# Two fused cross attentions on one core: x, context and weights turned before the launch, and layer two's maxima fused with their row term

## The reference

```python
# layer one (L0)
q = emb @ Wq + bq;  k = latent @ Wk + bk;  v = latent @ Wv + bv
w = softmax(q @ k.T / sqrt(512), axis=1)          # over the queries
x = w @ v + emb
n = (x - mean(x)) * rsqrt(var(x) + 1e-6);  x = n * gamma + beta
# layer two (L1)
Q = x @ Wq + bq;  K = ctx @ Wk + bk;  V = ctx @ Wv + bv
p = softmax(Q @ K.T / sqrt(512), axis=-1)
out = x + (p @ V) @ Wo + bo
```

## Time and profile before

| | |
|---|---|
| median of 3 runs | 739.02 us (738.49 to 739.14) |
| profiled execution, its own time | 739.57 us |
| span of the profile | 737.5 us, so 2.07 us lie outside it |
| PE busy | 690.4 us (94%) |
| DVE busy | 623.4 us (85%) |
| ACT busy | 422.5 us (57%) |
| POOL busy | 489.0 us (66%) |
| DMA | 49.50 MB, mean 67 GB/s |

### The profile page before, as it was taken

One profiled execution on the slowest core, in us unless ns is written; L12 is line 12 of the kernel. 1 busy time (PEld: TensorE's weight loads), 2 busy tenths in 40 slices (PEclk: granted clock), 3 DMA queues, 4 the chain that ended last, 5 costly groups with the idle time before them and its releaser, 6 DMA issues.

```text
span 737.5 us, 12580 instructions
## 1 busy us (share of the span) xinstructions
PE 690.4 (94%) x4107; PEld 596.5 (81%) x4107; DVE 623.4 (85%) x1282; ACT 422.5 (57%) x1009; POOL 489.0 (66%) x391
## 2 busy tenths in 40 slices
PE   8997989899998989999998999999899999989886
PEld 6875978788897878888797888889788878978775
DVE  4896797988979798897979889797989989797964
ACT  3644747556475656646574755647375574847432
POOL 0177758768484876858487685848669584857571
PEclk9999999999999999999999999999999999999999
DMA  8802004040300304040120404022040402101002
GB/s 287 284 1 86 2 10 134 1 142 0 133 9 34 108 0 142 0 142 0 49 93 0 142 0 142 0 65 77 0 142 0 142 0 91 51 0 58 1 1 114
DMA packets 30336, 49.50 MB, mean 67 GB/s; under 512 B 2160, under 2 KB 10352, under 8 KB 30320
## 3 DMA queue, kind: packets, MB, share of 16 engines
q1 hardware_dynamic: 30320, 49.29, 19.9%
HBM read 32.51 MB, written 16.78 MB: 67 GB/s over the span
## 4 chain that ended last, share of the span: by engine, by line
PE 55%; DVE 32%; ACT 5%; issue 4%; POOL 2%; DMA 1%; DVEq 0%; SPq 0%; POOLq 0%
PE bank L384 43%; PE bank L391 11%; DVE n L1003 6%; DVE neg L955 5%; DVE mx L949 3%; DVE top L952 3%; DVE stats L992 3%; DVE pc_lo L802 2%; DVE e L1109 2%; ACT e L702 2%; DVE wc_lo L802 1%; DVE x_odd L987 1%; DVE x_even L987 1%; ACT prod L709 1%; ACT wc_hi L631 1%
## 5 line engine op out<-in xcount | busy, mean ns | idle before, releaser
L1181 POOL TENSOR_TENSOR prod<-n,u_b 128x512 f32<-128x512 f32 x64 | 81.6, 1296 | 5.5 <-ACT prod L715 5.5
L800 DVE SCALAR_TENSOR_TENSOR y_lo<-bank,terms,y_hi 128x512 fp32r<-128x512 f32 x64 | 45.6, 748 | 37.5 <-ACT y_hi L629 37.5
L1210 POOL TENSOR_TENSOR r<-r,beta_b 128x512 f32<-128x512 f32 x60 | 75.7, 1289 | 0.0
L1203 POOL TENSOR_TENSOR r<-n,gamma_b 128x512 f32<-128x512 f32 x60 | 75.5, 1286 | 0.0
L1173 POOL TENSOR_TENSOR rstd<-var_eps,minus_half 128x2 f32<-128x2 f32 x32 | 22.4, 699 | 78.9 <-DVE var_eps L999 78.8
L629 ACT ACTIVATE y_hi<-bank,terms 128x512 fp32r<-128x512 f32 x64 | 42.0, 680 | 51.6 <-PE bank L384 51.5
L631 ACT ACTIVATE xT_hi<-bank 128x512 fp32r<-128x512 f32 x64 | 33.0, 605 | 67.0 <-PE bank L391 67.0
L702 ACT ACTIVATE e<-bank,neg 128x256 f32<-128x256 f32 x64 | 29.7, 469 | 52.7 <-DVE neg L955 52.7
L1142 POOL TENSOR_TENSOR cn_even_lo<-ctxn,cn_even_hi 128x1024 fp32r<-128x1024 f32 x8 | 19.2, 2394 | 56.3 <-ACT cn_even_hi L739 56.3
L384 PE MATMUL bank<-wvo_hi,pc_hi 128*128 128x512 f32 x128 | 52.2, 408 | 4.2 <-DVE pc_lo L802 4.2
L384 PE MATMUL bank<-xT_hi,wqk_hi 128*128 128x512 f32 x128 | 52.6, 411 | 2.0 <-DVE xT_lo L802 2.0
(11 more groups left out here) (197 smaller groups left out, 2514.4 us busy)
## 6 DMA issues: line engine op xcount, KB each, us to landing
out_dram<-r SPq DMA_DIRECT2D x15, 1024.0 KB, 5.1
x_even<-in_x_dram SPq DMA_DIRECT2D x8, 1024.0 KB, 7.1
...
x_odd<-in_x_dram SPq DMA_DIRECT2D x8, 1024.0 KB, 6.9
...
wq_sb<-in_L_xattn_Wq_dram SPq DMA_DIRECT2D x1, 1024.0 KB, 11.9
```

The source lines that it names most:

```text
L800: i = dve.scalar_tensor_tensor(dst, src, bias, high.bitcast(F32), ALU.add, ALU.subtract)
L1181: pool.tensor_tensor(prod[j % 2][:], N[:, j, :], u_b[1][:], ALU.mult).then_inc(prod_ready, 1)
L1203: pool.tensor_tensor(r[:, j, :], N[:, j, :], gamma_b[:], ALU.mult).then_inc(scaled_ready, 1)
L1210: pool.tensor_tensor(r[:, j, :], r[:, j, :], beta_b[:], ALU.add).then_inc(resid_ready, 1)
```

## The change

The host lays out transposed copies: `x_turned` and `ctx_turned` (per pair, partition = column), and Wq, Wk, Wv transposed; `columns` holds six bias vectors by partition. TensorE no longer turns x, ctx or weights. x arrives a second time as `x_raw` (1 MB a pair), ctx as `c_raw` (512 KB, in the buffer E1). ScalarE rounds `x_raw` in two halves (`round_xT`) and VectorE subtracts (`cut_xT`), both for the pair ahead and inside the previous iteration; ScalarE rounds `c_raw` (`round_cT`) and GpSimd subtracts (`cut_cT`). The bias vectors are products on TensorE with one column each (`term_columns`) in place of VectorE's dot products. In `maxima1` one tensor_scalar adds r1s and takes the maximum, writing into E1, and the exponential then reads E1. In GpSimd's order `row_products` 2, 3 moves behind `add_w_lo`, in ScalarE's `row_terms` 2, 3 behind wc. PSUM is used in rounds of 7 banks.

```diff
             def project(it, name, source, wqk, src):
                 dst = [begin(it, name, c) for c in range(KC)]
                 for k in range(KD):
-                    wait_emptied(pe, it, source, k)
+                    if source == "nT":
+                        wait_emptied(pe, it, "nT", k)
+                    elif k % 2 == 0:
+                        pe.wait_ge(xT_lo, it.times(2, k // 2 + 1))
...
+            def term_columns(it, L, wqT, wkT, bq):
+                dst = begin(it, f"t{L}")
+                columns = ([(wqT[:, :, k * P:(k + 1) * P], bk_col[L]) for k in range(KD)]
+                           + [(wkT[:, :, c * P:(c + 1) * P], bq) for c in range(KC)]
+                           + [(bk_col[L].unsqueeze(2).to_broadcast([P, KD, P]), bq)])
+                for n, (w, v) in enumerate(columns):
+                    for e in range(KD):
+                        mm = pe.matmul(dst[:, n:n + 1], w[:, e, :], v[:, e:e + 1], start=e == 0, stop=e == KD - 1)
+                end(mm, f"t{L}")
...
                 if it.front:
-                    transpose_inputs(it)
                     project(it, "y", "xT", WQK[0], XT)
-                if begin_it:
-                    prepare1a(it)
...
             def iteration(it):          # SyncE
                     sp.dma_start(XN[1 - it.parity][:], rows_of(x_rows, upcoming))\
                         .then_inc(x_loaded[1 - it.parity], 16)
-                    sp.wait_ge(filled[BANK["cT", KC - 1]], cT_filled)
-                    sp.wait_ge(cn_lo, cn_cut)
+                    sp.wait_ge(xT_lo, xT_cut)
+                    sp.dma_start(x_raw[:], whole_pair(x_turned, pair_after)).then_inc(x_raw_loaded, 16)
+                    sp.wait_ge(cn_lo, pair_after)
                     sp.dma_start(ctxn[:], rows_of(ctx_rows, upcoming)).then_inc(ctx_loaded, 16)
+                    sp.wait_ge(cT_lo, pair_after)
+                    if it.back:
+                        sp.wait_ge(filled[BANK["pt", 1]], pt_made)
+                    sp.dma_start(c_raw, whole_pair(ctx_turned, pair_after)).then_inc(c_raw_loaded, 16)
...
+            def round_xT(it, h, ahead):
+                act.wait_ge(x_raw_loaded, it.times(16, 16 + 16 * ahead))
+                act.activation(XT[0][:, 2 * h:2 * h + 2, :], x_raw[:, 2 * h:2 * h + 2, :], ACT.Copy)\
+                   .then_inc(hi["xT"], 1)
+            def round_cT(it):
+                act.wait_ge(c_raw_loaded, it.times(16, 16))
+                act.activation(CT[it.parity][0][:], c_raw, ACT.Copy).then_inc(hi["cT"], 1)
...
             def iteration(it):          # ScalarE
                 if it.back:
-                    row_terms(it, (2, 3))
                     for c in range(KC):
                         round_bank(it, "y1", c, Y1[0][:, c, :], bias=ccol[1][:, c:c + 1])
+                if more:
+                    round_xT(it, 0, 1)
+                if it.front:
+                    for b in range(2):
+                        round_bank(it, "wc", b, halves(WC[0], b))
+                if more:
+                    round_xT(it, 1, 1)
+                if it.back:
+                    row_terms(it, (2, 3))
...
+            def cut_xT(it, h, ahead):
+                dve.wait_ge(hi["xT"], it.times(2, 2 * ahead + h + 1))
+                dve.tensor_tensor(XT[1][:, 2 * h:2 * h + 2, :], x_raw[:, 2 * h:2 * h + 2, :],
+                                  XT[0][:, 2 * h:2 * h + 2, :].bitcast(F32), ALU.subtract).then_inc(xT_lo, 1)
...
             def maxima1(it):
-                s = ccol[1][:, KC:KC + 1]
                 dve.wait_ge(r1_ready, it.times(J, 0))
+                dve.tensor_scalar(r1s[:], r1[:], ccol[1][:, KC:KC + 1], None, ALU.add).then_inc(r1s_ready, 1)
                 for b in range(2):
                     wait_filled(dve, it, "s1", b)
+                    for tt in range(RT):
+                        q = b * RT + tt
+                        i = dve.tensor_scalar(E1[:, b, tt, :], at(("s1", b))[:, tt * M:(tt + 1) * M],
+                                              r1s[:, q:q + 1], LOWEST, ALU.add, ALU.max, accum_out=top1[:, q:q + 1])
...
                     q = slice(b * RT, (b + 1) * RT)
-                    dve.tensor_reduce(mx1[:, q], at(("s1", b))[:].rearrange("p (t m) -> p t m", t=RT), AX_X,
-                                      ALU.max).then_inc(mx1_ready, 1)
-                    dve.scalar_tensor_tensor(top1[:, q], r1[:, q], s, mx1[:, q], ALU.add, ALU.add)\
-                    dve.scalar_tensor_tensor(neg1[:, q], r1[:, q], s, top1[:, q], ALU.add, ALU.subtract)\
+                    dve.tensor_scalar(neg1[:, q], top1[:, q], -1.0, None, ALU.mult).then_inc(neg1_ready, 1)
...
+            def cut_cT(it):
+                pool.wait_ge(hi["cT"], it.times(1, 1))
+                pool.tensor_tensor(CT[it.parity][1][:], c_raw, CT[it.parity][0][:].bitcast(F32), ALU.subtract)\
+                    .then_inc(cT_lo, 1)
...
             def iteration(it):          # GpSimd
                 if it.front:
+                    cut_cT(it)
                     cut_ctx(it)
                 if it.back:
                     row_products(it, (0, 1))
                     if it.front:
                         scale_n(it)
+                if it.front:
+                    add_w_lo(it)
+                if it.back:
                     row_products(it, (2, 3))
                     if not it.front:
                         scale_n(it)
-                if it.front:
-                    add_w_lo(it)
```

311 lines of the change are left out of this document (125 added, 186 removed).

## The result

The change makes the kernel slower: 776.58 us median (773.49 to 777.91) against 739.08 us (738.49 to 739.46), a ratio of 1.050, 95% interval [1.047, 1.053]. The profiled execution took 773.49 us, with a span of 771.7.

A forecast was written before the change was run, and what follows sets the result against it. GpSimd's chain, alternating with VectorE, was taken to bound the pair: period 17.1 + 26.75 = 43.9. Span 737.5 - 3.5 + 13 x 1.25 - 3.9 = 746.4, so 748 us; likeliest 743 to 756, 8 in 10 722 to 757.

The forecast's parts named there:

- Start: Up to the third y: layer two's weight transposes and waits go, one-column products come; 3.5 us off, between 0 and 9.
- Term columns: TensorE's start: two sets of 28 one-column fp32 products, 0.11 us a record, 6 us a set (down to 3).
- w_lo to rstd: GpSimd's chain from the end of w_lo to the first rstd grows from 16.21 to 18.9 us.
- a cut of xT: VectorE's two xT cuts among GpSimd's products: each costs GpSimd 0.9 us, 1.8 for both (bounds 0 and 2.44).
- row products: row_products 2 and 3, moved behind w_lo on GpSimd, add 2.5 us to its chain.
- first `scale_n`: GpSimd, ready at 6.9 us after the start of y, waits for the store and starts at 10.7.
- from rstd to out 2: Both n, one more add and statistics, and pc_lo take 4.96 us from the first rstd to out 2.
- (a): Rival: n 2 and 3 precede cut_cT, or the store doesn't hold scale_n; period 42.05, time 724 us; chance 0.17.
- (b): Rival: xT cuts cost GpSimd nothing, VectorE or TensorE bounds; period 40.25 at best, about 700 us; chance 0.06.
- (d): Rival: x_raw load slows the store, or each xT cut holds GpSimd 1.22 us; 756 to 763 us; chance 0.08.
- (c): Rival: half of (a), in one of two iterations, or store landing in 4; period 43.0, 736 to 738 us; chance 0.12.
- maxima1: Fused row constants and maxima gain 2.5 us, between 1 and 4; pays only if GpSimd's chain is not the later.

The follow-up runs named there:

- e10: Changed kernel with term columns 64 wide, VectorE's Wqk cuts before the next xT cut, ScalarE's sums before u1 and wvo, 25 instead of 5 warm-up products: 765.0 us.
- e3: Changed kernel with the products of the term columns 64 columns wide (the same column repeated) instead of one: 768.1 us.
- e13: Changed kernel with two of the four blocks of every term column left out, so row constants are not the right ones: 763.3 us.
- e4: Changed kernel with VectorE's cuts of layer two's Wqk in iteration 0 ahead of the first cut of the next xT: 770.1 us.
- e9: Changed kernel with ScalarE, in the first iteration, summing the next x's row products before it rounds u1 and the two wvo banks: 773.4 us.
- e15: Changed kernel with eight 512-column products of TensorE into the unused eighth bank between out 1 and out 2: 773.2 us.
- e14: Changed kernel with a pair's store cut in four, each block behind its own out, and scale_n waiting for one block at a time: 749.7 us.
- e6: Changed kernel with GpSimd waiting for all four n before its cuts, and eight filling products of TensorE between out 1 and out 2: 761.0 us.
- e2: Changed kernel with the loop's VectorE cuts of xT_lo over 64 of 512 columns only, the rest left out: 760.9 us.

## Why the prediction was wrong

The direction was right, the time outside the range. The time forecast was 748 us, the likeliest range 743 to 756, and that for 8 in 10 722 to 757. Against the sum's span of 746.4 the profile has 771.7. The 25.3 us are 20.7 in the start, 5.9 in the period and -1.3 at the end.

**The step that failed is "Start": "I take 3.5 us off up to the third y".** It went 17.2 up. TensorE's preparations end at 79.76 instead of 58.81 in the two timelines, 20.9 later, by four parts (about 21 in sum):
- *Half clock, about 9.5 us, not in the sum at all.* The first Wqk took 9.44 for 7.14, y of pair 0 7.87 for 5.87, the row sums with the weighing 6.05 for 3.80, pr 8.32 for 5.84, the spread of the row constants 1.09 for 0.6. The first two come back in e10: y with wide columns (5.85 in e3 too), the first Wqk with a longer warm-up (7.17).
- *Term columns 14.0 us* where I had 12; a record took 0.12 to 0.13, not 0.11. (The 1.75 that I gave for 16 transposes is the time from one group's start to the next; the row says 1.91.) e13 confirms that the columns are paid in full.
- *Transposes taken away, -6.6 us*, by the starts of what followed them.
- *Waits, 4.1 us more*, of which 3.77 is pr 0, whose bank VectorE empties only behind the new cut of xT and wc_lo. The prediction looked at VectorE's new order in the loop and not in iteration 0. e4 takes this wait away.

Before, TensorE then had 7.6 us of transposes and waits ahead of the second y, so that y is only 12.8 later. But the second rstd of pair 0, which came 3.0 ahead of the second y, now comes 5.1 behind it, since it stands behind products that wait for ScalarE's sums, and those behind u1 and wvo (the 8.95 in the row at 81.08). Pair 1 takes 48.4 instead of 43.9: together the 17.2. e9's profile shows this second half (44.9), though its median does not tell it clear of noise. Of the 20.7 us e10 wins back 8.6 by edits of order, width and warm-up; how the rest divides between columns and clock is read from the timelines, and no run takes all the columns out, so that stays open.

**The steady pair was right in mechanism and in size.** At full clock the three pairs from 393.01 took 44.4, 44.1 and 44.0 (43.9 forecast). By terms: w_lo to rstd 19.0 (18.9); a cut of xT costs GpSimd 0.96 (0.9); row products 2.5 (2.5); w_lo at 17.1 to 17.3 (17.1); first `scale_n` at 10.8 to 11.0 (10.7); from rstd to out 2 4.9 to 5.2 (4.96). In these pairs `n` 2 and 3 ended at 2.1 and 4.7 (2.2 and 4.7). The mean of 44.34 is 0.44 more, from uneven pairs: those whose next out 2 falls into a half-clock stretch gain 1.5 us, those behind one give most back. e15 puts the net of that at 0.2; the rest stays in e15 too, where rstd to out 2 takes up to 5.4. TensorE's busy share came out at 89% (86 forecast): at half clock it is busy for longer.

**The rivals.** (a) had 42.05 for a store that doesn't hold `scale_n`, with w_lo at 15.3; e14 measures 42.24 and 15.3. But I had let `n` first stand for the same thing. e6 shows that it does not: GpSimd waits 1.2 us for both `n`, w_lo ends at 16.2 and the period is 43.3. (b) falls with e2, where shorter cuts gave 1.0 a pair. (d) had 756 to 763 us for a slower store (it landed in 5.2; 5.1 before) or a full hold of 1.22 (0.96): neither happened, and neither made the 776. (c) did not happen either: `cut_cT` started 0.04 ahead of the second rstd's end in every one of the 13 pairs.

**What a cut costs.** The two cuts cost GpSimd 1.9, and I had 1.8 from the row of an add. By the full block of the Trainium skill (SBUF — State Buffer, Who interferes with whom) it would be 2.44, an estimate from the row's 1.22. The trace agrees on who contends; the size was better taken from the row.

**maxima1.** Row constant, fused passes and `neg` run from 373.00 to 376.74, 3.7 us, of which 1.26 is the held r1s. Before it was 5.1, so 1.4 are gained (2.5 forecast, 1 to 4 as bounds). In the loop it doesn't matter, as rstd is late. The end came out 5.2 shorter (3.9).

**Not tested.** The seven banks in turn and the second x load, which I costed at nothing, were not tried alone; in the pairs at full clock the terms above leave 0.1 to 0.5 us for them.
